# A fused two-layer transformer kernel: the sorted expert rows in two groups, small stages in other slots of the steps, and products of the identity in the passes without pairs

## The reference

```python
x = L0_attn_x
x = x + _L0_attn_ref(_layernorm(x), Wq, Wk, Wv, g_scale)       # 16 heads of 8, q and k of unit length
x = x + _L0_ffn_ref(_layernorm(x), ...)                        # 8 experts of width 32, one for each row
x = x + _L1_attn_ref(_layernorm(x), w_q, w_k, w_v, w_o)        # 16 heads of 64, causal
x = x + _L1_ffn_ref(_layernorm(x), Wg, bg, W1, b1, W2, b2, gamma, beta)
```

```python
logits = x @ Wg + bg;  top2_vals, top2_idx = top_k(logits, 2);  scores = softmax(top2_vals)
y_e = gelu(x @ W1[e] + b1[e]) @ W2[e] + b2[e]
out = sum over the two chosen e of scores * y_e
return _layer_norm(x + out, gamma, beta)
```

## Time and profile before

| | us |
|---|---|
| median of 3 runs | 1639.59 (1637.74 to 1648.77) |
| the profiled execution, its own time | 1636.53 |
| its span, first to last instruction | 1634.8 |
| PE busy in the span | 1327.0 (81%) |
| DVE busy | 934.6 (57%) |
| ACT busy | 851.8 (52%) |
| POOL busy | 600.4 (37%) |
| mean granted TensorE clock | 0.917 of full speed |

### The profile page before, as it was taken

The page is one execution under the profiler, slowest core; times in us unless marked ns, Lnnn a source line. Parts: engine busy times, 40 slices in busy tenths (PEclk is TensorE's granted clock), DMA queues, the critical chain, the costliest instruction groups (busy, mean ns, idle before and its releaser), DMA issues.

```text
span 1634.8 us, 27815 instructions
## 1 busy us (share of the span) xinstructions
PE 1327.0 (81%) x9189; PEld 798.3 (49%) x9189; DVE 934.6 (57%) x3262; ACT 851.8 (52%) x1642; POOL 600.4 (37%) x768
## 2 busy tenths in 40 slices
PE   3878888988888789889988988988888884599970
PEld 1223444554455445545445444544555553488860
DVE  5355755565756576656555764555554654265655
ACT  3665665656565556555654665444424531255533
POOL 1010322233253335333423442235325444265554
PEclk7878999999999999989998999899979987699985
DMA  7060990000000000000000000001010000212222
GB/s 288 1 229 1 8 3 1 1 7 8 1 14 8 7 1 21 1 7 3 19 1 8 8 8 1 7 8 59 8 43 36 1 11 22 90 54 55 58 90 104
DMA packets 63051, 53.17 MB, mean 33 GB/s; under 512 B 39752, under 2 KB 49488, under 8 KB 62656
## 3 DMA queue, kind: packets, MB, share of 16 engines
q1 hardware_dynamic: 58592, 42.47, 13.2%
q0 software_dynamic: 4320, 8.92, 1.6%
HBM read 20.56 MB, written 30.81 MB: 31 GB/s over the span
## 4 chain that ended last, share of the span: by engine, by line
PE 59%; DVE 17%; ACT 14%; issue 7%; POOL 2%; DMA 1%; POOLq 1%; SPq 0%; DVEq 0%; ACTq 0%
PE scores L1529 10%; PE work L1469 8%; PE outs L1675 7%; PE outs L1548 6%; DVE scores L1085 5%; ACT a_buf L824 5%; PE work L1578 4%; PE scores L1498 3%; DVE ra L1078 3%; PE scores L1662 3%; PE work L1561 3%; ACT ra L830 3%; PE outs L1860 2%; ACT rsum L836 2%; PE work L1559 2%
## 5 line engine op out<-in xcount | busy, mean ns | idle before, releaser
L1085 DVE CUSTOM_DVE_ANT_0 scores<-scores,mask_qk 128x512 f32<-128x512 f32 (+3 forms) x512 | 239.3, 520 | 240.8 <-PE scores L1498 238.1
L824 ACT ACTIVATE a_buf<-scores 128x1024 f32<-128x1024 f32 x256 | 248.0, 1026 | 110.7 <-PE scores L1662 101.4
L676 POOL TENSOR_SCALAR_AFFINE_SELECT big<-big 128x256 f32<-128x256 f32 x256 | 100.9, 407 | 541.5 <-ACT big L818 540.7
L818 ACT ACTIVATE big<-scores 128x1024 f32<-128x1024 f32 (+1 forms) x192 | 169.2, 882 | 231.0 <-PE scores L1529 224.5
L1529 PE MATMUL scores<-ra 64*128 64x512 f32 (+3 forms) x1536 | 188.8, 352 | 47.2 <-ACT a_buf L824 33.0
L686 POOL TENSOR_TENSOR big<-big 128x768 f32<-128x768 f32 x64 | 118.6, 1854 | 191.2 <-PE work L1561 191.0
L1529 PEld LDWEIGHTS scores<-ra 64*128 64x128 f32 x1536 | 124.4, 193 | 109.4 <-ACT a_buf L824 42.3
L1548 PE MATMUL outs<-big 128*64 128x512 f32 (+3 forms) x1024 | 164.8, 449 | 2.2 <-DVE yT L1109 2.2
L1675 PE MATMUL outs<-a_buf 128*16 128x512 f32 x1024 | 148.4, 655 | 8.6 <-DVE wqkv_lo L1032 4.9
L1109 DVE TENSOR_TENSOR yT<-outs,rsum 128x512 f32<-128x512 f32 x64 | 44.3, 692 | 148.4 <-ACT rsum L841 148.4
L1548 PEld LDWEIGHTS outs<-big 128*64 128x64 f32 x1024 | 64.2, 137 | 115.9 <-issue 103.4
(11 more groups left out here) (216 smaller groups left out, 2600.7 us busy)
## 6 DMA issues: line engine op xcount, KB each, us to landing
sorted_rows<-xrows SPq DMA_DIRECT2D x33, 520.0 KB, 6.8
big<-sorted_rows SPq DMA_DIRECT2D x71, 65.0 KB
a_buf<-in_w SPq DMA_DIRECT2D x2, 2048.0 KB, 8.2
a_buf<-choice_rows SPq DMA_DIRECT2D x16, 256.0 KB, 4.9
a_buf<-in_x SPq DMA_DIRECT2D x8, 256.0 KB, 2.9
x_rows<-x SPq DMA_DIRECT2D x8, 256.0 KB, 2.0
ra<-x_rows SPq DMA_DIRECT2D x8, 256.0 KB
out<-a_buf SPq DMA_DIRECT2D x8, 256.0 KB, 2.0
```

Source lines behind the costliest of these rows:

```text
L818: activation(prob1(g, i), d[:, :, 0:256] if i == 2 else d, ACT.Exp, scale=SCALE1).then_inc(unit_free("pair", g, i), 1)
L824: activation(prob0(c)[:, i * 1024:(i + 1) * 1024], unit_wait(act, "cosine", c, i), ACT.Exp).then_inc(unit_free("cosine", c, i), 1)
L1085: return v.tensor_tensor_reduce(scores_, scores_, mask_qk[:, SEQ - width:SEQ], -1.0, 3e38, ALU.add, ALU.min, neg_max[:, qt, j:j + 1])
```

## The change

1. **Two groups.** `EARLY` holds batches 0 to 4 in 47 tiles, `LATE` batches 5 to 7 in 31 tiles, together 78. Each has its region of `sorted_rows`, its counts and its tables. `tables(EARLY)` stands at the end of step (6, 7), `tables(LATE)` in the tile loop behind tile 27.
2. **Pass 8 is cut to its first step** (`early_steps`). What batch 7 still needs is put into the tile loop by constants `AT_...`: the projection and the variances behind tile 1, standardizing at 4, transposes at 7, logits and routing at 10, ranks at 16, slots and gates at 18, two indirect DMAs at each of tiles 21 to 24. The tile loop starts when the values of the last pair are done (SP waits for `out_full[0]`).
3. **Finish inside the loop.** From tile 53 on, every fourth tile carries one batch of `EARLY` through the finish; behind the loop stand three batches.
4. **SP's order**: the loads of `x3_rows` stand ahead of the load of tile 47; the ten loads of the chosen rows of `EARLY` behind the load of tile 54 and ahead of that of tile 55.
5. **One bank each** for `xt_bank` and for `expert_out` (both in `outs`), since `work` is used by batch 7.
6. **Steps dealt anew.** A new slot (W) behind `values0` of the cosine before; every slot mostly one small stage; `values0(c0)` ahead of the projection of k (passes from 0 on); at p = 3 the cosines c0 behind slot X, and on ACT behind score unit 1. `parts_copied` goes to the end of steps 0, 2 and 4, `inverse_norms` and `unit_rows` from step 6 to 7, `slots1` from 5 to 6, the weight folding from step (-2, 0) to (-2, 6).
7. **`idle_products`**: products of the identity with itself into a bank that nobody reads, 10 behind `cosines(c0)` and 10 behind `cosines(c1)` in the steps of passes -2 and -1, 40 in step (-3, 7).

```diff
+EARLY = Group(0, 5, 0, 0)
+LATE = Group(5, BATCH, EARLY.end, EARLY.blocks)
...
+GELU_STEP = 3
...
+def early_steps():
+
+    for o in steps():
+        if o.i < LAST_PASS or o.p == 0:
+            yield o
...
+AT_PROJ, AT_ROWS, AT_SECOND, AT_ROWS_T = 1, 4, 6, 7
+AT_LOGITS, AT_RANK, AT_SLOTS, AT_SEND, AT_TABLES = 10, 16, 18, 21, 27
+FINISH_AT, FINISH_EVERY = LATE.tile + 6, 4
...
+        xt_bank, y_bank = outs[:, 1, 0:P], outs[:, 0, 0:DIM]
...
+            sp.wait_ge(rows_sent, 16 * CHOICES * TILES * EARLY.last)
+            sp.wait_ge(tables_ready, 1)
+            sp.wait_ge(out_full[0], ALL_PAIRS)
+            sorted_tiles(0, AT_TABLES)
+            sp.wait_ge(x3_ready, BATCH)
+            sp.dma_start(x3_rows[LAST_T], x3[:]).then_inc(kept, 16)
+            sorted_tiles(AT_TABLES, EARLY.end)
+            sp.wait_ge(kept, 16 * BATCH)
+            for b in range(BATCH):
+                sp.dma_start(x3_kept(b), x3_rows[b]).then_inc(x3_back, 16)
             sp.wait_ge(rows_sent, 16 * CHOICES * TILES * BATCH)
...
+            sp.wait_ge(tables_ready, 2)
+            sorted_tiles(EARLY.end, EARLY.end + RING)
+            chosen_rows(EARLY)
+            sorted_tiles(EARLY.end + RING, ALL_TILES)
+            finished_rows(EARLY)
+            sp.wait_ge(y_full, ALL_TILES)
+            chosen_rows(LATE)
+            finished_rows(LATE)
...
+            def idle_products(n):
+
+                for _ in range(n):
+                    mm(outs[:, 0, 0:P], ident_r[:], ident_r[:], start=True, stop=True)
...
                 if o.pair(-1) is not None:
                     values1(o.pair(-1), (0, 1))
-                if o.cosine(0) is not None:
+                if o.cosine(0) is not None and p != GELU_STEP:
                     cosines(o.cosine(0))
+                if s is not None and o.i < 0:
+                    idle_products(10)
                 if o.pair(-1) is not None:
                     values1(o.pair(-1), (2, 3))
...
                 if o.pair(1) is not None:
                     max_transposed(o.pair(1))
+                if o.cosine(0) is not None and o.i >= 0:
+                    values0(o.cosine(0))
                 if o.pair(2) is not None:
                     project("k", 1, o.pair(2))
                 if o.cosine(1) is not None:
                     cosines(o.cosine(1))
-                if o.cosine(0) is not None:
+                if s is not None and o.i < 0:
+                    idle_products(10)
+                if o.cosine(0) is not None and o.i < 0:
                     values0(o.cosine(0))
...
                 if p == 7 and h is not None:
+                    if s is None:
+                        idle_products(40)
                     group_operands(h, 0)
...
             def expert_out(n):
 
                 pe.wait_ge(hidT_ready, n + 1)
-                if n >= 2:
-                    pe.wait_ge(y_step, n - 1)
+                if n >= 1:
+                    pe.wait_ge(y_step, n)
+                else:
+                    pe.wait_ge(out_free[0], ALL_PAIRS + 1)
...
+                if n == AT_PROJ:
+                    projection_out("projB", LAST_T, range(4, PAIRS))
+                if n == AT_ROWS_T:
+                    pe.wait_ge(rows_ready["l1"], BATCH)
+                    transposes(xn, "xnT", LAST_T)
+                if n == AT_LOGITS:
+                    logits1(LAST_T)
+                if n == AT_RANK:
+                    ranks1(LAST_T)
```

605 lines of the change are left out of this document (348 added, 257 removed).

## The result

The changed kernel took 1666.3 us (median of 4 runs, 1657.5 to 1678.3) against 1643.5 us for the kernel before beside it: a ratio of 1.0173, 95% interval 1.0102 to 1.0243, so 28 us slower (17 to 40); the medians alone are 22.8 apart. The prediction was 1594 us with a range to 1632 and a chance of 0.07 for slower. The profiled execution had a span of 1671.8 us against 1634.8, +37.0.

The account below looks back on a forecast made before the run. PE's own work plus short waits was taken to bound passes 0 to 5, and PE the loop. Gap, finish and loop -7.7, dealing -35, products -2.5 made -45 us: span 1589.6, predicted 1594 us, range 1564 to 1632.

Parts of the forecast that it names:

- Part A: Gap ahead of the tile loop: first product with W1 comes at 1364.7 instead of 1402.2, -37.5 us.
- Part B: Finish behind the loop: five batches fewer at 4.46 us each, -22.3 us.
- Part C: Tile loop: seven more tiles, batch 7's stages, inserted finish work, DMAs and loads lengthen it, +52.1 us.
- five batches of sums and variances: DVE in the tile loop: 2.65 us each, 1.45 over the free time; 7.2 us in all.
- +3.5 for ACT: Tile loop: two more table loads of 1.28 us and five standardizations on ACT, +3.5 us (0 to 11).
- Part D: Passes, steps dealt anew: four kinds of PE waits shrink, -5.3 us a pass; -35 us together.
- the lost cover: Passes, steps 0 and 7: with `values0` moved, c1's exponential is late for the next score unit 0, +1.5 us.
- Rival 2: Passes: dealing anew only moves the waits, since ACT's exponentials bound PE's order; about -9, 1620 us; chance 0.17.
- Part E: Passes without pairs: identity products cost 32 us, 10.5 hidden in waits, full clock gives back 24; -2.5 us.
- Rival 3: Passes without pairs: products do nothing for the clock and lie open, +40 for -2.5; 1636 us; chance 0.07.
- Rival 4: Tile loop: single banks make every tile wait, from 0.8 us a tile, +62; 1656 us, slower; chance 0.07.
- Rival 1: Tile loop: inserted stages are covered by idle time of DVE, ACT and POOL, 20 us vanish; 1574 us; chance 0.15.

Follow-up runs that it names:

- all mendings but the last: Changed kernel without products, early batches' finish one tile later, two banks from tile 24, x3 and chosen-row loads spread: 1608.8 us, ratio 0.9842 to the kernel before.

## Why the prediction was wrong

The sum was -45 us; the profiled execution had +37. The 82 us between them are four terms by their stages: the products 25, the dealing 25 (of 35, less 10 found), the loop 31.5, the gap and the finish together 1.

**Part A (-37.5): right, -33.8.** The product with W1 comes 7.3 us behind the last values (1373.4 to 1380.7), not 5.2, and the values themselves end 1.6 us later after the start of pass 7. In the timeline of PE ahead of it:

```profile
1377.26 0.45 PE L2003 MATMUL outs<-ident_r,big 128*128 128x128 f32 x1 [2.98 <-DMA big<-sorted_rows]
1378.53 0.45 PE L2003 MATMUL outs<-ident_r,big 128*128 128x128 f32 x1 [0.83 <-DVE x_lo L1528]
1379.75 0.45 PE L2003 MATMUL outs<-ident_r,big 128*128 128x128 f32 x1 [0.77 <-DVE x_lo L1528]
```

PE waits 2.98 us for SP's load, and the second and third transpose, which share one bank with the first, wait 0.83 and 0.77 us for DVE's read of it. The prediction used the single bank as a cost in the steady loop and forgot it at its start.

**Part B (-22.3): right, -25.0, but not at its price.** The three batches left come 2.6 to 2.7 us apart and not 4.46, since the change also puts the next batch's sum ahead of `shift` there. The prediction did not see this; at 4.46 the finish would have been some 3.6 us longer (an estimate: two distances of 1.8).

**Part C (+52.1): the list was right, one term mis-sized and one wait missing; +83.6.** Foretold stops that came: a load wait ahead of tile 55's transpose (4.9 us, the longest of the DMA line; 7.5 was forecast), the stop for x3 ahead of tile 47, POOL's transfers at four tiles. The loads were +10 and +0 in the sum, and spreading them gave back 11.5. The term that failed is "five batches of sums and variances, 1.45 over, 7.2 in all", with +3.5 for ACT. It priced each inserted stage by its own length against 1.2 us of slack, as though a stage could start when DVE reached it. The finish inside the loop cost 34.2 us (the run with the finish behind), 27.0 more than the 7.2; the rest of the list measured 32.7 for 28.2, and the two make the miss of 31.5. The missing item is a wait inside the finish's own chain: `shift` in DVE's order comes before POOL can have the deviation, because POOL is behind a scatter (0.98), an add (1.27) and the power itself (1.04). The change adds a wait, and what is queued behind it on DVE is the low part that PE needs. The rows for this were there: the finish of the kernel before has the same wait, 1.13 us a batch, inside the 4.46 of the earlier trace rows (the line below), and the diff put the four stages at distances of one tile from each other, 2.38 us. Moving the stages by one tile gave 19.4 us, and two banks 20.8.

```profile
1606.81 0.16 DVE L1434 SCALAR_TENSOR_TENSOR shift<-mean,rstd 128x4 f32<-128x4 f32 x1 [1.13 <-POOL rstd L669]
```

**Part D (-35): about half, and not by its mechanism.** -5.3 a pass was the sum of four waits removed. They were removed or made smaller, and the undisturbed pass went from 156.9 to 156.6 us. The step that failed is the lost cover, put at 1.5 us. The credit for `values0` ahead of k, "covers its 0.37 us in 8 steps, -3.0", came (2.9 us). But what it had covered was read for the exponentials only: behind k also stand the operand transposes of `group_operands`, which need the bank that DVE's copy of k's low part frees. That put 4.0 us a pass back, and `parts` 1.5. What was left, 2.0 us less waiting, met 1.7 us more busy time of PE, whose cause no run shows. Most of what was taken from PE's waits came back as a wait for the next bank in line. Rival 2 (0.17) said this, and gave -9; what was found is -16 to -20 in the ratios and -10 in the stages of the first table, 5 to 7 of it ahead of pass 0, where the prediction had put nothing. The rest is at most partly in fewer disturbed passes, and its cause stays open. Part D's two further terms, a third of the other slow-clock time (-5) and `tables(EARLY)` (+2), were not measured apart.

**Part E (-2.5): wrong, +22.8.** Three steps failed. The price: 0.10 us a product was taken from transposes of the same identity; at the full clock ten took 1.33, at half clock 2.40 us, where eight transposes took 1.26. Together 49.5 us for the 32 forecast, of which 39.9 added to PE's busy time. The cover: 17.0 us of idle time were taken over and not 10.5, better than forecast. The gain: full clock was to give back 24 us. Without products the clock was 0.81 to 0.85 in eight executions dealt anew and 0.82 in the old order in the changed kernel, against 0.77 in the one profile that the prediction read; with them it was 0.84 to 0.86. Whether that 0.77 belongs to the old kernel or to its one execution is open, but a gain from 0.77 to full clock was not there to be had. Rival 3 (0.07) had the mechanism and, at +40, more than its price. The Trainium skill (TensorE: Matmul & The Clock Gate, Back-to-back issue gap) gives 81 ns for one product of 128 columns in a stream with its weight load. In these traces that comes near for bf16 (ten in 0.73 us) and not for fp32r (ten in 1.33). The same page (Weight-path perf modes) has the fast weight load for 128 weights of a type that is not FP32; the weight loads here took 20.5 us for 320 in bf16 and 44.6 us for 320 in fp32r, which is in line with it, though the profile does not show which way a weight was loaded. No run here separates the weight's share from the rest.

**The rivals.** Rival 4, single banks at +62, comes closest to the measured time but not by its mechanism: a steady tile took 2.3 to 2.4 us (tiles 47 to 52). The single banks matter only when something else stops. Rival 1 (covered stops) fell. Each rival was one part going wrong; the result took 2 and 3 together and a third of 4 (two banks gave back 20.8 of its 62). The prediction gave them 0.31 in sum as alternatives, and nothing to their falling together. All three leaned on the same doubt: PE's free time was counted as free for the stage put there, without asking who is late next.

## What to carry to other kernels

When a chain over several engines (DVE, POOL, DVE, ACT, DVE) is laid into a tuned loop, cost each link not by its length but by when its input is ready at its place in each in-order queue. A link placed too early stops everything queued behind it: here one more tile of distance for four stages was worth 19 us. When a wait is removed by moving cover, look up everything that this cover stood in front of: a pass with four waits removed or shortened was as long as before. Big loads issued in one block put their whole length ahead of the next small load; dealt out one or two at a time they cost 11.5 us less here. Work added to keep the clock up has to be cheaper than the clock it buys, and is measured against the kernel that has the other changes in it.

## What the runs showed of the hardware

- A product of 128 columns in fp32r took 0.13 us in a block of ten at the full clock and 0.24 at half; in bf16 0.07 and 0.125. A transpose of the same size by the same identity, 0.11 and 0.16, is no price for an fp32r product at half clock.
- Passes of identical instructions come in two lengths, 156.6 to 157.4 us with 3 to 7 us at half clock, and 159 to 165 us with 10 us or more. The changed kernel without products had passes 1 and 2 short and 3 and 4 long; with two banks in the loop, which doesn't touch the passes, 1 and 2 were long and 3 and 4 short. A difference of ten or fifteen microseconds between two single executions of this kernel means nothing unless the stages are compared.
- The stops of PE in the loop brought its clock down to 1.2 of 2.4 GHz for some microseconds behind them: 64 us at half clock in the changed loop, 16 in the loop before, 13 with all mendings but the last. Removing 16.7 us of waits of DVE shortened the loop by 19.4.
- Two indirect transfers a tile took POOL to 4.1 us a tile in a loop of 2.2, and DVE's gating stood 5.2 and 5.1 us at tiles 23 and 25; with one transfer a tile both stands were gone. By the trace no engine released them.
- A wait of DVE for POOL's inverse deviation took 2.4 us where POOL had only the scatter ahead of it and 3.6 us with an add of 1.27 us there as well.
